# One stage for keys, values, queries and feed-forward weights, with the keys' parts turned by DMA transposes

## What is computed

```python
q = (layernorm(x) @ Wq + bq);  k, v = split(cond @ Wkv + bkv)
q = fq_sym(q * 32**-0.5, per head and token); k = fq_sym(k, per head and key)   # 127 steps
v = fq_sym(v, per column, over all keys)
attn = fq_unsigned(softmax(q @ k.T), per row)                                  # 255 steps
x = x + (attn @ v) @ Wp + bp
# feed-forward: W1, W2 and the activations rounded in blocks of 32 to 8 bits
# with one exponent a block (mx_quant); gelu between; residual and two layernorms
```

## Time and profile before

| | us |
|---|---|
| median of 3 runs | 2850.61 |
| lowest, highest | 2848.39, 2852.79 |
| the profiled execution | 2848.46 |
| its span | 2846.7 |
| weights, queries, keys and values (until attention's first DMA issue) | 648.27 |
| attention's first and last chunk on VectorE | 660.1, 2508.7 |
| feed-forward part, first matmul of it to the end | 2524.4 to 2846.7 |

### The profile page before, as it was taken

How to read it: one execution, slowest core, us unless ns; L and a number is a source line. 1 busy time by engine, 2 the same in 40 slices (tenths; PEclk the granted TensorE clock), 3 DMA queues, 4 the chain that set the end, 5 groups by cost and what they waited for, 6 DMA issues and landing times. The chain is left out here.

```text
span 2846.7 us, 54272 instructions
## 1 busy us (share of the span) xinstructions
PE 2213.0 (78%) x20003; PEld 1185.6 (42%) x20020; DVE 2507.0 (88%) x3665; ACT 1993.3 (70%) x1859; POOL 1403.7 (49%) x1772
## 2 busy tenths in 40 slices
PE   0378999995787787878787888777888777868776
PEld 0234555542444444444444444444444444433333
DVE  8675666666999999999999999999999999957887
ACT  1123444444888888888888888888888888855554
POOL 0000111114657667576676676766757767653321
PEclk9698999996778878787888887877877888778989
DMA  6112233319999999999999999999999999970000
GB/s 245 68 26 96 92 129 129 111 69 187 179 198 186 206 192 190 201 186 194 203 183 211 187 193 203 185 198 194 189 204 186 204 201 182 176 205 4 15 15 26
DMA packets 1422976, 444.75 MB, mean 156 GB/s; under 512 B 1378280, under 2 KB 1393640, under 8 KB 1421712
## 3 DMA queue, kind: packets, MB, share of 16 engines
q1 hardware_dynamic: 1311664, 402.10, 69.8%
q10 hardware_dynamic: 111168, 40.93, 7.2%
HBM read 80.41 MB, written 43.77 MB: 44 GB/s over the span
## 5 line engine op out<-in xcount | busy, mean ns | idle before, releaser
L778 DVE TENSOR_SCALAR_CACHE_REDUCE arena<-a_ps_s 128x1281 f32<-128x1281 f32 (+1 forms) x1280 | 1822.9, 1489 | 26.0 <-PE a_ps_s L726 10.6
L835 ACT ACTIVATE arena<-arena,a_bias,a_row_scale 128x3328 uint8<-128x3328 f32 (+1 forms) x512 | 1559.8, 3047 | 242.9 <-POOL a_bias L893 201.9
L726 PE MATMUL a_ps_s<-arena,a_q_rep 96*128 96x512 bf16 (+2 forms) x3840 | 1186.6, 429 | 378.5 <-DVE arena L778 345.9
L726 PEld LDWEIGHTS a_ps_s<-arena,a_q_rep 96*128 (+1 forms) x3840 | 309.0, 108 | 809.5 <-DVE arena L778 460.5
L739 PEld LDWEIGHTS a_ps_o<-a_v_head,a_nT 128*128 128x128 f16 x13056 | 521.6, 102 | 257.2 <-issue 141.3
L900 POOL CAST a_nT<-arena 128x1664 int16<-128x1664 uint8 x256 | 402.2, 1571 | 447.4 <-DMA arena<-arena 445.6
L739 PE MATMUL a_ps_o<-a_v_head,a_nT 128*128 128x32 f16 x13056 | 512.6, 182 | 26.2 <-POOL a_nT L901 23.6
L901 POOL CAST a_nT<-arena 128x1664 int16<-128x1664 uint8 x256 | 403.5, 1576 | 0.0
L471 POOL TENSOR_TENSOR kv_parts<-kv_rest,kv_parts 128x512 bf16<-128x512 f32 (+1 forms) x51 | 59.0, 1158 | 576.9 <-ACT kv_parts L586 576.9
L591 ACT ACTIVATE kv_stage<-kv_ps_t 128x1024 bf16<-128x1024 bf16 (+1 forms) x51 | 51.4, 1008 | 204.7 <-PE kv_ps_t L508 204.7
L499 PE MATMUL kv_ps_k<-wkv,kv_ctxT 128*128 128x512 f32 (+1 forms) x408 | 184.6, 595 | 0.0
(11 more groups left out here) (157 smaller groups left out, 1944.0 us busy)
## 6 DMA issues: line engine op xcount, KB each, us to landing
k_parts_transposed<-kv_stage SPq DMA_DIRECT2D x10, 1920.0 KB, 7.8
kv_ctx<-in_ctx_dram SPq DMA_DIRECT2D x10, 1280.0 KB
v<-arena SPq DMA_DIRECT2D x10, 1280.0 KB
arena<-k_parts_transposed ACTq DMA_DIRECT2D x48, 240.1 KB, 3.8
arena<-in_L_ffn_W_dram SPq DMA_DIRECT2D x2, 4096.0 KB, 20.5
arena<-k_parts_transposed ACTq DMA_DIRECT2D x48, 160.1 KB, 3.8
a_v_raw<-v ACTq DMA_DIRECT2D x32, 208.0 KB
a_q_rep<-q_transposed ACTq DMA_DIRECT2D x48, 128.0 KB, 5.3
```

The lines of the kernel that those rows point to most:

```text
L726: last = nc.tensor.matmul(ps_s[:, b, n0:n0 + w], q, k_parts[0:3 * HD, slot, start[c] + n0:start[c] + n0 + w], start=True, stop=True)
L778: nc.vector.tensor_scalar(s_row[:, u, start[c]:start[c] + size[c]], ps_s[:, (u + c) % 2, 0:size[c]], 1.0, None, ALU.mult, ALU.max, accum_o ...
L835: nc.scalar.activation(out, s_row[:, u, keys_of_half[half]], ACT.Exp, scale=row_scale[:, u, 0:1], bias=bias[:, u:u + 1], accum_out=zsum[:, ...
```

## The change

The first three stages become one, `prepare`. It has one loop over 25 pairs of key tiles and the tile of 4 keys, then one over the 16 query tiles.

- Keys' parts. TensorE's 12 turns and ACT's two copies of them are gone. SP issues a DMA transpose of the three parts for each tile (`turn_keys`), 12 blocks of 128 x 128, from SBUF to SBUF, and stores `stage` for two tiles at a time. `parts` has two buffers; ACT may write one again when its transpose has landed.
- VectorE's `split` writes the rounded keys as int8 (one multiply, no rounding step). The rest after the first part is formed on POOL, which so has two subtractions a tile. In a pair VectorE does both splits, then takes and compares the values of each tile. ACT does both parts of both tiles and then the absolute values.
- Weights. W1 and W2 come in 8 pieces of 2048 numbers a partition; one piece takes four tiles (powers after tile 1, bytes after tile 2, values after tile 3, the two halves turned by TensorE and copied by ACT at tiles 4 and 5, counted from the piece's start).
- Queries. The moments of the first 8 tiles of x are taken beside key tiles 32 to 39, and they are normalised in place beside tiles 41 to 48; the other 8 in the query loop.
- Values. After the last key tile POOL reduces the largest values, VectorE inverts them, and the values, kept in SBUF, are rounded to 8 bits head by head beside the queries: even heads by VectorE's multiply, odd ones scaled by POOL in three parts and rounded by ACT. ACT then writes them as f16 and its queue stores them to DRAM in the order in which attention reads them. For that the value tiles below 26 are projected from every second column of a pair (`columns_of`).
- Attention. POOL's scaling and rounding and VectorE's inversion are gone; a head's values come by one load of 3264 bytes a partition.

```diff
+            def turn_keys(t):
+                g = t // 2
+                sp.wait_ge(lo_ready, t + 1)
+                after_first(sp, k_stored[g % 2], 16 * (g // 2))
+                sp.dma_start_transpose(stage[:, g % 2, :, t % 2 * P:(t % 2 + 1) * P],
+                                       parts[:, t % 2].rearrange("p s c -> p (s c)")).then_inc(kT_turned[t % 2], 16)
...
+            for t in range(KT):
+                differences(t)
+            pool.wait_ge(vmax_done, KT + 1)
+            nc.gpsimd.partition_all_reduce(v_scale[:], v_scale[:], P, bass.bass_isa.ReduceOp.max).then_inc(reduced, 1)
+            pool.wait_ge(inv_ready, 1)
+            for h in range(1, H, 2):
+                for part in range(V_PARTS):
...
+                if 2 * g + 2 < KT:
+                    copy_c(2 * g + 2)
+                first_part(2 * g)
+                if 2 * g + 3 < KT:
+                    copy_c(2 * g + 3)
+                second_part(2 * g)
+                if 2 * g + 1 < KT:
+                    first_part(2 * g + 1)
+                    second_part(2 * g + 1)
+                for t in tiles:
+                    absolute_values(t)
+                    for half in range(2):
+                        if piece_at(t, 4 + half) is not None:
+                            copy_weights(piece_at(t, 4 + half), half)
...
+            for t in range(QT):
+                if t == 2:
+                    roots(1)
+                if t + 2 < QT:
+                    copy_c(KT + t + 2)
+                copy_query(t)
+                if t >= 1:
+                    store_values(t - 1)
+                round_values(t)
+            store_values(QT - 1)
...
+            dve.wait_ge(wkv_loaded, 32)
+            split_bias()
+            for t in range(KT):
+                if t % 2 == 0:
+                    for of_pair in range(t, min(t + 2, KT)):
+                        split(of_pair)
+                take_values(t)
+                largest_value(t)
+                if piece_at(t, 1) is not None:
+                    powers(piece_at(t, 1))
+                if piece_at(t, 2) is not None:
+                    weight_bytes(piece_at(t, 2))
+                if piece_at(t, 3) is not None:
+                    weight_values(piece_at(t, 3))
+                if 0 <= t - X_TILE < HALF_Q:
+                    moments(t - X_TILE)
```

## The result

| | before | after |
|---|---|---|
| median of 4 runs, us | 2851.7 | 2815.3 |
| lowest, highest | 2848.4, 2856.2 | 2811.5, 2815.6 |
| span of the profiled execution | 2846.7 | 2813.7 |
| attention's first DMA issue | 648.3 | 624.0 |
| first and last chunk on VectorE | 660.1, 2508.7 | 636.4, 2475.2 |

The ratio is 0.9868, 95% interval 0.9851 to 0.9885: the change takes 36 us off. The forecast had the sign right, but a gain of 10 us by its own sum (2848.5 to 2839; 12 to 13 against the median here), a third of it; the time lies inside the stated range of 2790 to 2900 and outside the forecast's own, 2820 to 2860. Between the two profiles (33.0 us by span) 24.3 us lie ahead of attention and 8.7 us from there to the end.

A forecast was written before the change was run, and what follows sets the result against it. Attention was taken as VectorE's, so everything hung on when it starts: 509 + 40 + 85 + 14 + 10 = 658 us, 10 later; 2848.5 + 10 - 20 = 2839 us. Range 2790 to 2900, its own 2820 to 2860.

The forecast's parts named there:

- 51 tiles: Key tiles: pairs with weights 302 us, four pairs with moments 67, five with normalising 81, last tile 8; 458 us.
- to the third query's turn: Start of queries: VectorE's small steps take turns with POOL's scaling of odd heads; 40 us, 20 without that exclusion.
- the rest, cold projections among it: Later queries: 11 intervals 85 us, 14 for last roundings, store and stage change, 10 for slower projections after TensorE's pauses.
- given back from there on: Attention: VectorE's waits of 9.2 us in 2 times and 10.6 us in 9 go; -20 us (-9 to -20).
- The price of POOL's scaling: Start of queries: POOL's 24 pieces of 1.34 us hold VectorE's small steps; 40 us with the hold, 20 without.
- the layout of a pair of tiles: Key-tile pair: VectorE's splits and the chain over ACT and POOL, 12.95 us, plus 2.06 from VectorE-POOL exclusion: 15.0 us.
- The two long waits: Attention: VectorE's waits for the first exponent and for ACT held by its DMA issues, 9.2 us, go.
- The short ones: Attention: 10.6 us in 9 short waits for TensorE, at rows where ACT issues the next head's loads, go.
- rival 2: Key tiles and queries: each TensorE pause drops its clock to 1.2 GHz; 2.4 us for 26 pairs, +73, 2912; chance 0.25.
- Rival 1: Key tiles and queries: POOL doesn't hold VectorE; -52 and -20, 2767, with half of it 2803; chance 0.22.
- Rival 3: Key tiles: DMA transposes come later than the splits; 3191 at 16 us a tile, 3176 at 801 us; chance 0.02.
- Rival 4: Key tiles: TensorE sets 14.6 us a pair, 380 us in all, ACT's chain and POOL's hold hidden; 2755, chance 0.04.

## Why the prediction was right or wrong

The sum's terms against the profile after:

| | predicted | measured |
|---|---|---|
| first split of keys | 33 | 31.05 |
| 51 tiles | 458 | 432.0 |
| VectorE waiting for TensorE in them | 6 | 5.0 |
| reduction and inversion | 12 | 11.1 |
| to the third query's turn | 40 | 37.2 |
| the rest, cold projections among it | 85 + 14 + 10 | 107.6 |
| attention starts | 658 | 624.0 |
| given back from there on | 20 | 8.7 |

The measured terms come from the rows at 31.05, 468.10, 479.20, 516.43 (TensorE's third turn of queries) and 623.98 us; the 5.0 us are the sum of VectorE's 8 waits for keys.

**The start, the reduction and the queries** were right within 3 us each. That ACT's rounding stands in the loop of the queries is shown by its move: 34 us. The projections at the lower clock were counted in the right place too. The price of POOL's scaling was not: 20 us were put in for it, and leaving it out gave 13; the 40 us came out at 37.2 with other parts of that stretch longer.

**The step that failed is the layout of a pair of tiles**, from which the 458 us of the 51 tiles were built; they measured 432.0, which is 26 of the 34 us by which attention starts earlier than forecast. It gave 3.40, 4.92, 4.54 and 2.16 us for the first split, the second, to the first maximum and the second tile, 15.0 together. The first pair measured 3.40, 4.47, 4.34 and 1.98: 14.2, and 0.8 x 25 = 20 us. The mechanism is what the prediction said: VectorE's steps with two inputs in SBUF wait for POOL's instruction, as the run without the low part shows. Its size was off, by the turn it gave POOL and by the chain. The layout let POOL wait behind VectorE's multiply and run until 4.23 us after the first split; in the trace POOL's row began when its operand was there (2.61), stretched by only 0.15, and ended at 3.92. The hold was 1.07 + 0.54 us a pair and not 2.06 (0.45 us less), and the chain over ACT and POOL, 3.98 + 2.16 without it, came to 3.80 + 1.98 (0.36 us less). The pairs with bytes and values added 4.45 us and not 4.66, and the five that normalise came to 15.1 on the mean and not 16.2, 0.3 more than the layout explains: together some 3 of the remaining 6 us. The other 3 are not laid out here.

**Attention** was the second failure, in the other direction: 8.7 us and not 20, just under the stated lower end of 9. The two long waits, 9.2 us, went as said; the prediction put them to the work on the values and to ACT's issues, and no run tells these apart. The short ones were put to the loads of values because ACT issues them in the same rows as those of the keys. The rows couldn't tell the two apart, and the loads that the change left alone were the cause.

**The rivals.** By the prediction's own chances the range leaves out 0.29 (0.11 + 0.04 + 0.02 + 0.12) and not 2 in 10, and the 2.4 us a pair of rival 2 has no row that it is worked out from (1.96 us is the row's). Rival 1 (VectorE isn't held) is wrong on the mechanism, though the time lies between its half case, 2803, and the forecast. Rival 2 (the clock) fails in the tiles, 0.97 of full clock, and holds in a part of the queries (0.83 over all of them), where the sum had it. Rival 3 falls with the landing of a tile's 12 blocks, 4.1 us at the median of 51 and 5.8 at most. By the figure for one block on the VectorE page of the Trainium skill ("VectorE: DVE Perf Modes", The three transpose paths) they would have taken 15.7 us, an estimate; the trace doesn't agree for blocks that go in one transfer. Rival 4 (the pairs are TensorE's) is wrong for the changed kernel; pairs of 14.6 us needed ACT's order changed, once for those without weights and once more for those with powers.

Of the signs that the prediction named, the first add near 33 us, the pairs of 17 to 20 and 15 to 16 us (17.2 to 18.8, then 14.6 to 16.6), the long rows beside POOL's and no row of attention over 9 us were there. The turns of the queries were 8.1 us on the mean, against 7.8. Attention's first chunk came at 636.4 us and not near 670, and one sign of a wrong forecast came true: attention kept its short waits, 8.0 us in 11 where it had 10.6 in 9.

## What to carry to other kernels

When a change gives one queue of an in-order engine more to do, write out what stands directly behind each wait in it: two moves in ACT's list, with no work taken out, were worth more than the change itself (26 and 34 us, against 36). Two engines that exclude each other are priced by a timeline of the very pair, with the start of each instruction set by its operand; a rule of turns that was laid over it made more than half of an error of 0.8 us, and that twenty-five times. And before a stall is put to a transfer, ask which of the transfers in that place the change touches.

## What the runs showed that was not expected

- VectorE's first step with two inputs in SBUF, met by a row of short POOL instructions that follow each other without a gap, waited 6.95 and 7.56 us, some 18 of 0.386 us, and only then did the two alternate. With pieces of 1.33 us the first step waited 1.0. The SBUF page of the Trainium skill ("SBUF — State Buffer", Who interferes with whom) calls the shared ports an exclusive lock and says, of VectorE's two-port modes, that whoever issues first has them for the whole instruction. For the pieces of 1.33 us the trace agrees with such a lock; for the short ones it doesn't, as the wait is of 18 instructions and not of one. Why VectorE isn't let in between them stays open.
- The hold goes both ways: in the run with the absolute values first, POOL's subtraction of 1.16 us took 3.03 us where VectorE's step of 2.28 us with two inputs lay beside it.
- The same attention, in eleven kernels, took 1833.5 to 1841.8 us from its first to its last chunk, with 3 to 10 us of short waits: in one profile a smaller difference than this there tells nothing of a change.
